# A two-layer graph kernel: six blocks of the second aggregation held back and multiplied between the steps of the norm chain, their masks made and stored there, and the reading of z, the global maximum and the last group's steps put in another order

## What is computed

```python
A = adj + eye;  d = rsqrt(A.sum(axis=1));  An = d[:, None] * A * d[None, :]
h = relu(An @ (x @ W1) + b1);  x = layernorm(x + An @ (h @ W2) + b2)
# attention, for each head i
x_norm = _ln(x, g1, b1);  h = x_norm @ ff0_w[i].T
e = leaky_relu(h @ attn_w[i, :c] [:, None] + h @ attn_w[i, c:] [None, :])
atten = softmax(where((adj > 0) | eye, e, NEG), axis=1)
att = _ln(atten @ h + x, g2, b2)
h_next = h_next + elu(att @ ff1_w[i].T) / K
# and at the end
x = layernorm(x + h_next)
```

## Time and profile before

| | us |
|---|---|
| median of 3 runs (1058.07 to 1059.05) | 1058.78 |
| the profiled execution | 1058.95 |
| its span, first to last instruction | 1057.2 |
| PE busy | 988.1 (93%) |
| DVE busy | 698.4 (66%) |
| ACT busy | 495.6 (47%) |
| POOL busy | 114.5 (11%) |

### The profile page before, as it was taken

The page is one execution under the profiler, slowest core; times in us unless marked ns, Lnnn a source line. Parts: engine busy times, 40 slices in busy tenths (PEclk is TensorE's granted clock), DMA queues, the critical chain, the costliest instruction groups (busy, mean ns, idle before and its releaser), DMA issues. The chain is left out here.

```text
span 1057.2 us, 9226 instructions
## 1 busy us (share of the span) xinstructions
PE 988.1 (93%) x2592; PEld 477.7 (45%) x2592; DVE 698.4 (66%) x1249; ACT 495.6 (47%) x709; POOL 114.5 (11%) x146
## 2 busy tenths in 40 slices
PE   5788999999999999999869999999999999999992
PEld 4333444444644444444655444444544444454541
DVE  0567766654355433444828767788779999888977
ACT  3433332211200000001257765879668698878773
POOL 0011111111040000000710000101010101001012
PEclk8999999999999999999869999999999999999997
DMA  9999999999386999996023132222222232222211
GB/s 350 428 426 426 427 428 424 425 423 381 133 307 249 380 375 377 381 381 249 1 61 100 60 100 67 68 95 70 89 70 81 89 100 90 100 70 91 90 50 40
DMA packets 62219, 226.03 MB, mean 214 GB/s; under 512 B 4513, under 2 KB 44129, under 8 KB 52065
## 3 DMA queue, kind: packets, MB, share of 16 engines
q1 hardware_dynamic: 57056, 208.56, 51.4%
q10 hardware_dynamic: 5120, 17.01, 4.0%
HBM read 205.59 MB, written 19.96 MB: 213 GB/s over the span
## 5 line engine op out<-in xcount | busy, mean ns | idle before, releaser
L1200 PE MATMUL ps<-colbuf,stat 128*128 128x512 f32 x992 | 439.0, 598 | 27.3 <-DVE diag L760 26.8
L1200 PE MATMUL ps<-T,Yw 128*128 128x512 f32 x1024 | 446.8, 595 | 11.1 <-DVE T L918 11.1
L918 DVE SCALAR_TENSOR_TENSOR T<-T,mring 128x2048 f32<-128x2048 f32 x128 | 292.8, 2289 | 70.4 <-ACT T L577 69.9
L577 ACT ACTIVATE T<-Rrow,small,ratio 128x1024 f32<-128x1024 f32 x256 | 301.2, 1230 | 67.7 <-PE ps L1200 67.5
L1200 PEld LDWEIGHTS ps<-T,Yw 128*128 128x128 f32 x1024 | 194.7, 191 | 249.1 <-issue 229.6
L1200 PEld LDWEIGHTS ps<-colbuf,stat 128*128 128x128 f32 x992 | 186.4, 191 | 249.9 <-issue 219.3
L497 ACT ACTIVATE W<-W 128x4096 f32<-128x4096 f32 (+30 forms) x32 | 66.1, 2067 | 147.1 <-DMA W<-in_adj 147.1
L516 ACT ACTIVATE stat<-xw_g 128x128 f32 (+1 forms) x32 | 9.9, 310 | 197.8 <-PE ps L1200 155.9
L799 DVE TENSOR_SCALAR mtile<-colbuf 128x4096 uint8<-128x4096 f32 x30 | 69.7, 2322 | 10.4 <-DMA mask<-mtile 8.3
L795 DVE TENSOR_TENSOR colbuf<-colbuf,ident 128x128 f32 (+1 forms) x26 | 7.6, 292 | 91.8 <-DMA colbuf<-in_adjT 91.8
L720 DVE TENSOR_TENSOR W<-W,colbuf 128x3712 f32<-128x3712 f32 (+28 forms) x29 | 62.3, 2148 | 0.1
(11 more groups left out here) (161 smaller groups left out, 590.3 us busy)
## 6 DMA issues: line engine op xcount, KB each, us to landing
colbuf<-in_adjT SPq DMA_DIRECT2D x58, 2048.0 KB, 12.9
mring<-mask SPq DMA_DIRECT2D x128, 256.0 KB, 2.6
mask<-mtile ACTq DMA_DIRECT2D x32, 512.0 KB, 10.0
Rrow<-s_src SPq DMA_DIRECT2D x9, 512.0 KB, 4.3
W<-in_adj SPq DMA_DIRECT2D x2, 2048.0 KB, 14.9
W<-in_adjT SPq DMA_DIRECT2D x2, 2048.0 KB, 13.3
out<-final SPq DMA_DIRECT2D x5, 512.0 KB, 4.1
W<-in_xT SPq DMA_DIRECT2D x8, 256.0 KB, 6.8
```

Of the source, the lines that this page charges most:

```text
L577: last = act.activation(T[:, c % TS, j, :], Rrow[:, g % 2, :], ACT.Relu, scale=ratio[:, c * JB + j:c * JB + j + 1], bias=small[:, 8:9])
L918: v.scalar_tensor_tensor(out=tile, in0=tile, scalar=1.0, in1=mring[:, c % TS, :, :].rearrange("p b n -> p (b n)"), op0=ALU.add, op1=ALU.mu ...
L1200: return pe.matmul(*args, skip_group_check=True, **kw)
```

## The change

Three parts.

1. **Second pass.** `LATE` is now 6: rounds of the loop fall from 6 to 5, and six blocks are multiplied bank by bank. Four of them are in `colbuf`; two more are loaded into `rowbuf` after turns 4 and 5, early in the pass (SP, ahead of the loop). PE takes `xw_g` itself as weights there, without the copy `stat`. For k = 0 and 1 it first multiplies five blocks, then the sixth; from k = 2 on, three blocks, the turning of sum k-1, three blocks, the nodes of k-2, the scores of k-3. DVE adds the identity to all six blocks first, makes one mask, and then one more in each of the rounds k = 0 to 4, between the moments and the normalising (`late_mask`). SP stores these six. Groups 6 and 7 have no mask between; they are normalised one behind the other, and POOL makes their `r2` together.
2. **Between the layers.** The first group's scores for head 0 are scaled, turned, stored and loaded already during the chain (`early_st`). The table for exp is loaded by a dummy activation before the chain. The maximum over partitions is made by PE and DVE (`span` turned, `highest`, `top_diag` times `ones`), not by POOL. Eleven z steps (`Z_WAITING`) stand ahead of the first chunk, five of them read by DVE (`Z_MOVED`), six by ACT; five are left among the chunks.
3. **End.** `final_shift` stands behind the last `tail_mix`, the first `final_rows` behind the last `tail_square` and the second behind the last exp on ACT; both `tail_write` stand behind the last `tail_norm`.

The core of the diff:

```diff
-        AHEAD = LATE = 2
-        ROUNDS = NI - 2
+        AHEAD = 2
+        LATE = AHEAD + RING
+        ROUNDS = NI - 3
...
+            for n in range(AHEAD):
+                sp.wait_ge(pe_block, RING + n + (1 + MASK_CREDIT))
+                sp.wait_ge(mask_made, RING + n + (1 + MASK_CREDIT))
+                sp.dma_start(late(n)[0], dram_block(adj_cols, late(n)[1])).then_inc(row_loaded[n], 16)
...
+            for n in range(LATE):
+                turn = B - LATE + n
+                sp.wait_ge(mask_made, turn + (1 + MASK_CREDIT))
+                sp.dma_start(dram_block(mask_dram, late(n)[1]), mtile[:, turn % SN, :]).then_inc(mask_stored[turn % SN], 16)
+            sp.wait_ge(early_stored, 16)
+            source_row(0, 0)
...
+            late_mask(0)
+            for k in range(NG - 2):
+                add_skip(k)
+                if k + 1 < LATE:
+                    late_mask(k + 1)
+                normalise(k)
...
+            add_skip(NG - 2)
+            add_skip(NG - 1)
+            normalise(NG - 2)
+            normalise(NG - 1)
...
+            for k in range(2, NG):
+                late_sums(k, range(LATE // 2))
+                turn_sums(k - 1)
+                late_sums(k, range(LATE // 2, LATE))
+                turn_nodes(k - 2)
+                if k == EARLY - 1:
+                    pe.wait_ge(early_ready, 1)
+                if k >= 3:
+                    sources(k - 3)
+                if k == EARLY:
+                    pe.transpose(ps[0:GB, 1, 0:P], early_st[:, :], ident[:, :]).then_inc(early_turned, 1)
```

More of the change, by code:

```diff
@@ L113, in build @@
         half = sb("half", [P, B], F32)
+        ones = sb("ones", [P, P], F32)
         d_all = sb("d_all", [P, B], F32)
@@ L362, in phase @@
                     if c == 6:
-                        if not (isinstance(q, int) and g == 0):
+                        if isinstance(q, int) and g == 0:
+                            sp.wait_ge(s_stored, 16)
+                        else:
                             sp.wait_ge(relu_made, at_turn(q * (G * NC) + g * NC))
@@ L1190, in _ @@
             tail_y(1)
-            elu(last_phase, 1, G - 1, 1, 0)
-            tail_write(0)
-            elu(last_phase, 1, G - 1, 1, 1)
+            for stage in range(2):
+                elu(last_phase, 1, G - 1, 1, stage)
             tail_norm(1)
-            tail_write(1)
+            for part in range(2):
+                tail_write(part)
         @block.tensor
@@ new lines, in late_sums @@
+            def late_sums(k, some):
+                for n in some:
+                    block, b = late(n)
+                    if k == 0:
+                        if n < AHEAD:
+                            pe.wait_ge(row_loaded[n], NI * 32 + 32)
+                        else:
+                            pe.wait_ge(col_loaded[n - AHEAD], 16 * (NI + 1 + ROUNDS))
+                        pe.wait_ge(own_ready, ROUNDS * RING + AHEAD + n + 1)
+                    last = multiply(ps[:, k, :], xw_g[:, b, :], block[:, cols(k, GW)], start=False, stop=n == LATE - 1)
+                if n == LATE - 1:
+                    last.then_inc(agg_done, 1)
@@ L1329, in multiply_z @@
-            def multiply_z(r):
-                if r >= 4:
-                    pe.wait_ge(z_read, r - 3)
-                for i in range(2):
-                    last = multiply(ps[:, 4 + r % 4, cols(i, 2 * C)], x1T[:, cols(2 * r + i)],
-                                    gff[:, :, :].rearrange("p k c -> p (k c)"), start=True, stop=True)
-                last.then_inc(z_done, 1)
-            for r in range(Z_EARLY):
-                multiply_z(r)
+            multiply_z(0)
+            multiply_z(1)
@@ L1339, in _ @@
+            sources(NG - 3)
             pe.wait_ge(mixT_ready, 1)
             for head in range(K):
-                last = multiply(ps[:, 3, cols(head)], mixT[:, head, :], gff[:, head, :], start=True, stop=True)
+                last = multiply(ps[:, 1, cols(K + head)], mixT[:, head, :], gff[:, head, :], start=True, stop=True)
             last.then_inc(mix_done, 1)
+            turn_nodes(NG - 2)
+            multiply_z(2)
+            turn_nodes(NG - 1)
+            sources(NG - 2)
+            sources(NG - 1)
@@ new lines, in _ @@
+            multiply_z(3)
+            pe.wait_ge(st_ready, 1)
+            pe.transpose(ps[0:K * B, 0, P:2 * P], st[:, 0:K, :].rearrange("p k b -> p (k b)"), ident[:, :]).then_inc(s_turned, 1)
+            multiply_z(4)
+            pe.wait_ge(span_ready, 1)
+            pe.transpose(ps[0:2 * K, 6, 0:P], span[:, :], ident[:, :]).then_inc(span_turned, 1)
+            multiply_z(5)
+            pe.wait_ge(top_step, 2)
+            multiply(ps[:, 7, 0:2 * K], ones[0:2 * K, :], top_diag[:, :], start=True, stop=True).then_inc(top_done, 1)
```

281 lines of the change are left out of this document (167 added, 114 removed).

## The result

The changed kernel takes **1039.34 us** (median of 4 runs, 1038.42 to 1041.23); the kernel before, run beside it, 1058.91 us (4 runs, 1058.07 to 1059.1). The ratio is 0.9819, with a 95% interval of 0.9806 to 0.9832: 19.6 us faster. The forecast was 1041.0.

A forecast was written before the change was run, and what follows sets the result against it. PE bounds nearly every slice except between the layers, where a serial DVE, POOL, PE, ACT chain waits. Gains of 12.3+2.6+2.1+1.0 = 18.0 us off 1058.95 give 1040.95, forecast 1041; range 1036 to 1049.

The forecast's parts named there:

- Start of the chain: End of the second pass: DVE begins the serial chain at 478.7 us, with 1 us (0 to 3) lost to late blocks.
- I cost them at nothing: Second pass: the two blocks loaded early, at about 323 and 330 us, add no time, as DMA share is 0.16 then.
- The round of DVE: Masked rounds of the chain: POOL's 1.35 us begins when the mask ends, so DVE and POOL set a 7.3 us pace.
- The price of masks in the chain: Chain between the layers: five rounds of 0.4 us over PE's pace and a longer last stage, some 4.5 us together.
- Rival (a): Chain: masks do not hold up POOL, PE sets a 6.9 us pace, chain ends 4.5 us earlier: 1036.5 us; chance 0.15.
- L930: End of the chain: this step, L863 in the kernel before, starts at 531.9 us, where it started at 536.40.
- L930 to the first chunk: Between the layers: PE starts the attention's first chunk 11.4 us after this step, at 543.3, with DVE's z copies ending last.
- The clock in the first chunk: Attention's first chunk: PE stands still some 4 us at most, its clock holds, and 2.1 us is gained.
- Rival (b): Clock falls in the chain's last stage, so work through the first chunk runs at half speed: 5 us, 1046; chance 0.18.
- In the stream: Attention chunks: five z steps remain where there were eight; three at 0.87 us give 2.6 us.
- The end: End region: last write up to 2 us earlier, 1 us given back for three close stores: 1.0 us (0 to 2).
- Rival (d): Late masks wait for their stores, which set the pace, making the kernel slower: 1059 us and more; chance 0.03.

## Why the prediction was right, and where its terms were off

Time, sign and main mechanism were right. The sum of 18.0 agrees with the 17.7 of the profiles and the 19.6 of the medians in part by errors of opposite sign: the round was too long and the stream and the end too small, the clock too good.

- **Start of the chain, forecast 478.7, found 481.03**, but in a late execution: in four other profiles with the same order up to there 478.60 to 479.54, and the first turned sums at 477.92 to 478.86 where 478.4 was forecast. So the 1 us allowed for the landing (0 to 3) was of the right size. Its reason was not: "I cost them at nothing" is wrong for the two early blocks. I read the share of DMA in 8 us (0.16), and neither in the 60 around them (0.59) nor behind them (0.97). PE waits 0.51 to 2.65 us for blocks in all ten profiles with both loads whole, and not at all with them small.
- **The round of DVE, forecast 7.3, found 6.9** (6.94, 6.87, 6.88, then 7.22 with the early scores, 6.88). The mechanism was right: POOL is held to the mask's end. The sum had 0.4 us too much: L894 to the mask 2.37, to POOL's release 2.32, to the normalising 1.22, to the next L894 1.03 are 6.94. So the 2.42 up to the mask's second step should have ended with the mask itself, the 1.4 for POOL counted its first operation again, though that ends with the mask, and 0.4 for DVE's own waits was 0.3. As PE's round is 6.92, the two are tied, and after two rounds PE waits for nodes no more until the last stage. The price of masks in the chain was put at 4.5 us against a chain at PE's pace; the short masks give 2.8 to 3.3. Rival (a) was wrong in its mechanism; 1036.0 us, near its time, came only with seven eighths of the masks not made.
- **L930, forecast 531.9, found 532.37.** Start 2.3 late and five rounds 2.4 short: right by cancelling, which is luck. The last stage waits for PE (1.75 us for the sums of group 7), and there it is the same: PE's first turned sums 480.35 for 478.4, and its last block at 522.97 for 523. In three profiles that started on time L930 is at 529.93, 530.47 and 530.86, so there the short rounds are a gain over the forecast.
- **L930 to the first chunk, forecast 11.4, found 11.43**, with DVE's copies of z last, as worked out. Gain ahead of the first chunk 11.77, forecast 12.3.
- **The clock in the first chunk, forecast 2.1, found 0.3.** The step that failed is "I take the clock as held". The wait of 3.66 us, less than half of the 8.17, was enough: the granted clock is 1.00 in the wait and 0.72 in the chunk's 6.07 us, and with work in the wait the chunk takes 4.30. Rival (b) had this loss but put the fall into the last turning, where PE never stood still long, and the clock was 1.00. Its 5 us were wrong; of the 2.1 us of its last part 1.8 came.
- **In the stream, forecast 2.6 us from three z steps, found 3.8** besides the clock (4.12 less 0.3). One more microsecond lies in PE's waits for the masked tiles in the attention: 11.1 us in 5 waits before, 8.2 of it the first; 5.6 in 4 now, 3.66 of it the first. Leaving the first out, 2.9 against 1.9. Why the later ones are shorter wasn't tested.
- **The end, forecast 1.0, found 2.0.** The 2 us by which the last write moves were right; "give back 1 us" for three stores close together was not, and no row had shown such a price. The last stores land in 2.3 us, and last write to end is 5.55 us against 5.42.
- **Rival (d)**, slower by the mask stores: the six late ones land in 2.7 us at the median, and no late mask waits. The 92.5 us of waits for stores are all ahead of the chain, in the full traffic of the pass, and were slack.

The Trainium skill (SBUF — State Buffer, "Who interferes with whom") says that the port pair shared by VectorE and GpSimd is an exclusive lock, and that with VectorE in a two-port mode whoever issues first has the pair for the whole instruction and the other is blocked. The five 2.14 us operations and the 0.27 us under the short mask agree with that for an operation that comes after DVE's, and so does the 1.09 us of the earlier trace rows with an exclusive lock; in which mode the mask's operation runs no run here tells. L469 in the run with the mask behind the normalising began 0.04 us ahead of the mask by the profile (490.81 against 490.85), and was held just the same, while the mask took 2.28 us as ever. So by such small differences of the starts one can't say who comes first.

## What to carry to other kernels

A load is only free if the DMA engines have room for all of it, so read their share over a stretch as long as the transfer and behind it, not in the slice where it is issued: here 0.16 in 8 us, 0.59 in the 60 around, 0.97 behind. The landing of the last tile varies from one execution to the next, and so does the name of the transfer that is waited for; a reading of one profile is worth little until a second one of the same loads agrees. A wait that is shortened is not yet a wait that is gone: ask what the clock does in what is left, and price the work behind it at both levels of the clock. Where two engines share a chain, put both rounds side by side to a tenth of a microsecond before pricing one of them; here 0.5 us of difference in a round (7.40 against 6.92) turned slack into a loss.

## What the runs showed that was not expected

- A wait of 3.66 us of TensorE was enough for the granted clock to fall to 0.50 as soon as work began again (0.50 in 544 to 546, 0.66 in 546 to 548, 1.00 from 548), after 40 us of solid work at full clock. With work in the wait it stayed at 1.00. A wait of 2.60 us for a block, after solid work too, was followed by 0.52, and one of 2.51 us by 1.00.
- The loss behind the same wait of 3.66 us was 1.77 us in six profiles and 2.9 to 3.1 in two.
- A GpSimd operation between 128x4 tiles took 2.14 us instead of 0.19 under a mask of 2.26 us, 0.27 under one of 0.39, and one of 1.01 us took 3.19 when it began 0.04 us before the mask.
- With the same loads, DVE's waits in the pass were 14.4 us for loads and 91.8 for stores in one profile, and 81.8 and 22.6 in another. The sum stayed between 99 and 108 us.
